# A graph network of five layers on one core: which pieces of the edge list two layers take when, and how many node steps fit beside them

## The reference, cut to what matters

```python
x = _layernorm(x + L0(x, edge_index))    # h = x + segment_sum(x[src], dst); elu(h @ W1 + b1) @ W2 + b2
x = _layernorm(x + L1(x, src, dst, ef))  # messages: mlp(x[src], x[dst], ef); segment_sum by dst; mlp
x = _layernorm(x + L2(x, edge_index))    # two SAGE layers, below
x = _layernorm(x + L3(x, W, src, dst, etypes))   # segment_sum(x[src] @ W[etype], dst), 16 types

def _sage_mean(h, src, dst, Wl, Wr, b):
    agg = segment_sum(h[src], dst)
    mean = agg / max(cnt, 1)
    return _l2norm(mean @ Wl + b + h @ Wr)
# L2: h = _sage_mean(x, first weights); batch norm over all nodes; relu;
#     out = _l2norm(_sage_mean(h, second weights) + x)
```

## Time and profile before

| | us |
|---|---|
| median of three runs | 8759.73 (8747.03 to 8762.27) |
| the profiled execution, device time | 8745.67 |
| its span | 8743.7 |
| PE busy, share of the span | 5411.1, 62% |
| POOL busy | 6302.1, 72% |
| DVE busy | 3367.5, 39% |
| ACT busy | 1499.6, 17% |
| POOL's gathers `G<-x_tab` (layer three), 1040 | 994.6 |
| POOL's gathers `G<-g_tab` (layer four), 1040 | 991.6 |

### The profile page before, as it was taken

How to read it: one execution, slowest core, us unless ns; L and a number is a source line. 1 busy time by engine, 2 the same in 40 slices (tenths; PEclk the granted TensorE clock), 3 DMA queues, 4 the chain that set the end, 5 groups by cost and what they waited for, 6 DMA issues and landing times. The chain is left out here.

```text
span 8743.7 us, 127149 instructions
## 1 busy us (share of the span) xinstructions
PE 5411.1 (62%) x29370; PEld 4179.4 (48%) x29371; DVE 3367.5 (39%) x7842; ACT 1499.6 (17%) x3432; POOL 6302.1 (72%) x6643
## 2 busy tenths in 40 slices
PE   4456766666666666667788768778877333333333
PEld 3445555555666666655555545444444222222222
DVE  3224444434444444444445434555554111111111
ACT  1111111111111111112222212233333100000000
POOL 6777777767777777767777752777766477777777
PEclk6556556557777777767878865888888555555555
DMA  3111111113333333334545424544444111111111
GB/s 79 34 34 35 35 35 34 35 37 100 97 98 97 97 98 97 99 99 110 118 111 118 113 61 128 138 145 137 140 140 117 38 30 30 30 30 30 30 30 29
DMA packets 555851, 676.47 MB, mean 77 GB/s; under 512 B 242261, under 2 KB 358003, under 8 KB 555019
## 3 DMA queue, kind: packets, MB, share of 16 engines
q0 software_dynamic: 212448, 268.01, 15.6%
q1 hardware_dynamic: 201194, 306.89, 11.8%
q10 hardware_dynamic: 141441, 93.34, 3.5%
HBM read 574.09 MB, written 93.56 MB: 76 GB/s over the span
## 5 line engine op out<-in xcount | busy, mean ns | idle before, releaser
L1919 PE MATMUL PAG<-OH,G 128*64 128x96 f32 (+1 forms) x10224 | 1573.8, 337 | 2284.0 <-DMA G<-rel_tab,IDX 984.9
L1919 PEld LDWEIGHTS PAG<-OH,G 128*64 128x64 f32 (+1 forms) x10224 | 1424.7, 204 | 2438.6 <-issue 2415.3
L1919 PE MATMUL PH<-HT 125*128 125x192 bf16 (+4 forms) x10742 | 1991.2, 314 | 303.9 <-DVE HT L1449 92.2
L832 POOL DMA_INDIRECT G<-rel_tab,IDX x1507 | 1421.8, 943 | 546.3 <-issue 459.7
L832 POOL DMA_INDIRECT G<-in_x,SRC x1525 | 1451.6, 952 | 481.9 <-issue 464.6
L832 POOL DMA_INDIRECT G<-far_tab,SRC x1527 | 1442.3, 945 | 485.0 <-issue 465.2
L1919 PEld LDWEIGHTS PH<-HT 125*128 125x128 bf16 (+4 forms) x10742 | 1275.7, 156 | 995.6 <-issue 355.2
L1411 DVE TENSOR_TENSOR AGG<-AGG,PAG 64x96 f32 (+2 forms) x852 | 211.2, 248 | 3169.0 <-PE PAG L1919 3148.1
L832 POOL DMA_INDIRECT G<-g_tab,SRC x1040 | 991.6, 953 | 582.7 <-issue 498.5
L832 POOL DMA_INDIRECT G<-x_tab,SRC x1040 | 994.6, 956 | 334.7 <-issue 315.0
L1919 PE MATMUL PAG<-OH,HT 128*128 128x96 f32 x3126 | 611.0, 376 | 524.5 <-ACT HT L1127 518.0
(11 more groups left out here) (222 smaller groups left out, 4438.9 us busy)
## 6 DMA issues: line engine op xcount, KB each, us to landing
HT<-x_parts SPq DMA_DIRECT2D x160, 468.8 KB
HT<-g_parts SPq DMA_DIRECT2D x160, 468.8 KB
GROWS<-rel_tab SPq DMA_DIRECT2D x4096, 0.2 KB
GROWS<-in_x SPq DMA_DIRECT2D x3584, 0.2 KB
HT<-src_rows SPq DMA_DIRECT2D x320, 160.0 KB
rel_tab<-STG ACTq DMA_DIRECT2D x200, 250.0 KB
GROWS<-far_tab SPq DMA_DIRECT2D x3072, 0.5 KB
GROWS<-rel_tab ACTq DMA_DIRECT2D x3072, 0.2 KB
```

Of the source, the lines that this page charges most:

```text
L832: pool.indirect_dma_start(out=G[:, h, j, 0:tabs[p].shape[1]], out_offset=None, in_=tabs[p], in_offset=bass.IndirectOffsetOnAxis(ap=numbers ...
L1919: return nc.tensor.matmul(dst, lhsT, rhs, start=start, stop=stop, skip_group_check=True)
```

## The change

Four things, all in layers three and four, and one in the preparation.

- **Order of the supers.** A new function `super_at` says which piece of the edge list a step takes: step 28 and 29 now take supers 130 and 131, and steps 130 and 131 take 28 and 29, which are "held". POOL's gathers, DVE's one-hot matrices, the window starts and SP's rows go by it. With this unit 34 has its straight edges at step 30, unit 7, which the held supers touch, has them only behind step 131, and the units below 34 and above 7 that waited for the last two supers have theirs by step 130.
- **Batches.** They are spread over 118 steps and not 126 (`supers - 14` for `supers - 6`); the last stands in step 117. The last pairs of cells are summed on PE at the start of step 118, and DVE adds the last window in step 119, behind its beats. Units that need the last window are free from step 120 and no longer only behind the last super.
- **Beat places.** Layer four has four places a step, layer three still three (`BEAT_SLOTS`). The fourth stands at the step's end, behind the second batch.
- **DVE's starts of windows** are read two at a time, every second step, in place of four every fourth.
- **Preparation.** Nine limits are checked in place of five, with nine more `link` steps, so the counts that engines wait for rise by nine.

By the new tables `rest` has 8 beats in layer three and 15 in layer four. Up to the sum of super 117 PE has in layer four 160 batches and 344 beats, where it had 150 and 326.

```diff
-ROWS_READY, COUNTED_READY, PREP_READY, TABLES_READY = 71, 85, 92, 100
+ROWS_READY, COUNTED_READY, PREP_READY, TABLES_READY = 80, 94, 101, 109
...
+HELD = 28
+HELD_UNIT = 7
...
+BEAT_SLOTS = {2: 3, 3: 4}
...
+def super_at(p, s):
+    if p not in CELL_LAYERS:
+        return s
+    early = SUPERS_OF[p] - 2
+    return {HELD: early, HELD + 1: early + 1, early: HELD, early + 1: HELD + 1}.get(s, s)
...
-        due = min(total, -(-total * (s + 1) // (supers - 6)))
+        due = min(total, -(-total * (s + 1) // (supers - 14)))
...
-            needs[u] = (min(at, supers), windows)
-            free[u] = at if at < supers else supers
+            if u < HELD_UNIT:
+                at = min(at, HELD)
+            elif u == HELD_UNIT:
+                at = supers
+            elif u == apart - 1:
+                at = HELD + 2
+            else:
+                at = min(at, supers - 2)
+            needs[u] = (at, windows)
+            free[u] = at
...
-            free[u] = step_of.get(BATCHES * windows, supers) + 1
+            free[u] = step_of.get(BATCHES * windows, LAST_BATCH_AT[p] + 2) + 1
...
-        for _ in range(3):
+        for _ in range(BEAT_SLOTS[p]):
...
# PE, cell_layer
+                    if s == LAST_BATCH_AT[p] + 1:
+                        for e in range(pairs - LAG[p], pairs):
+                            sum_cells(e)
                     beats(by_step[s][0])
...
-                for e in range(pairs - LAG[p], pairs):
-                    sum_cells(e)
+                    for now in by_step[s][3:]:
+                        beats(now)
                 beats(rest)
...
# DVE, cell_layer
+                    if s == LAST_BATCH_AT[p] + 2:
+                        add_cells(p, windows - 1, s)
+                    if s >= LAST_BATCH_AT[p] + 2:
+                        windows_before = windows
-                if windows_before:
-                    dve.wait_ge(window_added, WINDOWS_BEFORE[p] + windows_before)
+                dve.wait_ge(window_added, WINDOWS_BEFORE[p] + windows)
                 add_straight(p, supers - 1, starts[supers - 1], D)
-                add_cells(p, windows - 1, supers)
                 beats(rest)
```

More of the change, by code:

```diff
@@ L94 @@
 CELL_LAYERS = {2: (132, 35), 3: (132, 35)}
+HELD = 28
+HELD_UNIT = 7
+assert HELD % 2 == 0 and SEGMENTS[0][0] <= HELD_UNIT < SEGMENTS[0][1]
 CELL_SUPERS = SLOTS
@@ L136 @@
 BATCHES_AT = {p: batches_by_step(p) for p in CELL_LAYERS}
+LAST_BATCH_AT = {p: max(s for s, batches in enumerate(at) if batches) for p, at in BATCHES_AT.items()}
 def cell_schedule(p):
@@ L283, in gnn_kernel @@
         REGULAR_I = sb("REGULAR_I", [1, 1], I32)
-        CHECKS = sb("CHECKS", [1, 2, 5])
+        CHECKS = sb("CHECKS", [1, 2, 9])
         DST_TAB = HT[:, N - SORTED * UNITS // 2:N].bitcast(F16).rearrange("p (w u) -> p w u", u=UNITS)
@@ L711, in some_rows @@
                     if at % AT_ONCE == 0:
-                        starts[:] = row_starts(sp, row_registers, p, SP_SUPERS[p][k] // 2, e)
+                        starts[:] = row_starts(sp, row_registers, p, super_at(p, SP_SUPERS[p][k]) // 2, e)
                     row(sp, p, k % ROW_BUFS, e, starts[at % AT_ONCE])
@@ L820, in _, with gathers @@
         def _(pool):
-            def gathers(p, s, base, by_rows=()):
+            def gathers(p, s, base, by_rows=(), edges_of=None):
                 numbers = IDX3 if p == 4 else SRC
@@ L828, in gathers @@
                     pool.wait_ge(summed, base + s + 1)
-                filled = GROUP - 1 if s in by_rows else filled_chunks(s)
+                t = s if edges_of is None else edges_of(p, s)
+                filled = GROUP - 1 if s in by_rows else filled_chunks(t)
                 for j in range(filled):
-                    c = s * GROUP + j
+                    c = t * GROUP + j
                     pool.indirect_dma_start(
@@ L835, in gathers, with layers @@
                     ).then_inc(gathered[h], 16 * (GROUP - j if j == filled - 1 else 1))
-            def layers(supers, base, rows):
+            def layers(supers, base, rows, edges_of=None):
                 for p in range(LAYERS):
@@ L848, in layers @@
                     for s in range(0 if p else SHARED, supers[p]):
-                        gathers(p, s, base[p], rows[p])
+                        gathers(p, s, base[p], rows[p], edges_of)
             even, even_base = [SUPERS] * LAYERS, [SUPERS * p for p in range(LAYERS)]
@@ L860, in _ @@
             with pool.If(regular > 0):
-                layers(SUPERS_OF, BASE, by_rows)
+                layers(SUPERS_OF, BASE, by_rows, super_at)
             with pool.If(regular < 1):
@@ L1284, in _ @@
             link(nc.vector.tensor_reduce(CHECKS[:, 0, 1:2], HT[0:1, 0:SORT_SUPERS], AX.X, ALU.max))
-            limits = [COLS - 1, 0] + [UNIT * apart - 1 for _, apart in CELL_LAYERS.values()] + [P]
+            limits = [COLS - 1, 0] + [UNIT * (apart - k) - WIN for _, apart in CELL_LAYERS.values() for k in (0, 1)]
+            limits += [UNIT * (HELD_UNIT + 1) - WIN, -UNIT * HELD_UNIT, P]
             for k, (supers, _) in enumerate(CELL_LAYERS.values()):
-                link(nc.vector.tensor_reduce(CHECKS[:, 0, 2 + k:3 + k], SPANS[0:1, 0:supers], AX.X, ALU.max))
+                link(nc.vector.tensor_reduce(CHECKS[:, 0, 2 + 2 * k:3 + 2 * k], FIRST[0:1, 0:supers], AX.X, ALU.max))
+                link(nc.vector.tensor_reduce(CHECKS[:, 0, 3 + 2 * k:4 + 2 * k], FIRST[0:1, 0:supers - 2], AX.X, ALU.max))
+            held = CHECKS[:, 0, 6:8]
+            link(nc.vector.tensor_reduce(held[:, 0:1], FIRST[0:1, HELD:HELD + 2], AX.X, ALU.max))
+            link(nc.vector.tensor_reduce(held[:, 1:2], FIRST[0:1, HELD:HELD + 2], AX.X, ALU.min))
+            link(nc.vector.tensor_scalar_mul(held[:, 1:2], held[:, 1:2], -1.0))
             for k, limit in enumerate(limits):
@@ L1359, in _ @@
             dve.wait_ge(prep_products, MOST_COUNTED)
-            link(nc.vector.tensor_reduce(CHECKS[:, 0, 4:5], MOST_P, AX.X, ALU.max))
+            link(nc.vector.tensor_reduce(CHECKS[:, 0, 8:9], MOST_P, AX.X, ALU.max))
             link(nc.vector.tensor_tensor(CHECKS[:, 0, :], CHECKS[:, 1, :], CHECKS[:, 0, :], ALU.subtract))
@@ L1840, in cell_layer @@
                 for s in range(supers):
-                    if s % SLOTS == 0:
-                        for k, w0 in enumerate(starts_of(dve, registers[s // SLOTS % 2], s)):
-                            starts[s + k] = w0
+                    if s % 2 == 0:
+                        pair = registers[s // SLOTS % 2][s % SLOTS:s % SLOTS + 2]
+                        starts[s], starts[s + 1] = starts_of(dve, pair, super_at(p, s))
                     if s:
@@ L1848, in cell_layer @@
                     if s + 1 < supers:
-                        one_hot((s + 1) % 2, DREL[:, s + 1, :]).then_inc(onehot_ready, 1)
+                        one_hot((s + 1) % 2, DREL[:, super_at(p, s + 1), :]).then_inc(onehot_ready, 1)
                     beats(by_step[s][0])
```

## The result

The changed kernel takes 8790.23 us (median of 5), the kernel before 8759.73: ratio 1.0038, 95% interval 1.0026 to 1.0049, so 33 us slower by the ratio and 30.5 by the medians. 8778 was predicted, within 8720 to 8812. The profiled execution has a span of 8770.5 us, 26.8 more than before; at 8772.3 us it is the fastest of the five, 18 under their median. Where these come from is read from the first gather of each layer (timeline, POOL alone, start and length in us) and from the addition of super 117's sum.

A forecast was written before the change was run, and what follows sets the result against it. POOL was taken to set the pace in layer three, PE in layer four; +1.5 - 20 - 37.3 + 74 = +18 us gave 8764 beside the profiled 8746, 8778 beside the median, range 8720 to 8812.

The forecast's parts named there:

- What bounds layer four: Layer four: PE sets the pace, with POOL waiting 75.1 us for slots that PE has not emptied.
- the second rival: Layer four: PE has room, so the 74 us of added work are nearly free: -56, 8704 us; chance 0.05.
- The ends: Ends of layers three and four: fewer units behind the last sum and POOL's pace in layer four gain 20 and 37.3 us.
- What is paid ahead of super 117's sum: Layer four up to that sum: batches, units, waits, edge rows and stores cost 74 us, bounds 20 and 120.
- waits that the new pattern adds: Layer four: roots on ACT ahead of the next batch's copies make PE wait, net 12 us, bounds -15 and +45.
- half of 19 x 3: Layer four: PE stands about 3 us in 19 steps with no batch between, at the clock's upper level; half is 28.
- The fifth rival: Layer four: ACT's roots and stores hold up batch copies, price 115 us for 74: +59, 8819 us; chance 0.09.
- Ten batches at 4.2 us: Layer four: ten more batches on PE ahead of super 117's sum cost 42 us, 37 if none waits.
- Edge rows: Layer four: PE's waits for rows that SP fetches grow by 5 us, bounds -20 and +25.
- Windows: Layer four: most of PE's 26.1 us of waits for window additions on DVE go.
- Stores: Layer four: units following sooner make ACT wait for stores of maps, 3 us more, bounds 0 to 20.
- Prologue: Ahead of the first sum: nine more small DVE steps cost 1.5 us, between 0.5 and 2.7.

The follow-up runs named there:

- e4: The changed kernel with a root in a step's first beat place in layer four moved behind the first batch's copies on ACT: 8786.12 us, ratio 1.0038 to before.
- e6: The changed kernel with no roots or flip (beats 2 to 5) in layer four's fourth place: 8788.47 us, ratio 1.0043 to before.
- e11: The changed kernel with three beat places for four in steps 103 to 117 of layer four: 8766.54 us, ratio 1.0013 to before.
- e2: The changed kernel with three beat places a step for four in layer four, batches still over 118 steps: 8737.76 us, ratio 0.9984 to before.
- e3: The changed kernel with layer four's batches over 126 steps again and three beat places: 8751.22 us, ratio 0.9992 to before.
- e1: The changed kernel with layer four's batches over 126 steps again, four beat places kept: 8786.08 us, ratio 1.0036 to before.
- e9: As e2, but DVE reads window starts by fours where no held super is in the group: 8736.59 us, ratio 0.9981 to before.
- e10: As e2, but with four beat places in layer four from step 118 on: 8743.33 us, ratio 0.9980 to before.
- e5: The kernel before with layer three's change alone, layer four's order and end as before: 8740.90 us, ratio 0.9986 to before.

## Why the prediction came out as it did

- **What bounds layer four** held: PE sets the pace there (POOL's waits 75.1 to 174.6 us), so the second rival, free work, fell; in layer three the moved batches cost nothing. By the Trainium skill (Perfetto Trace Analysis, Identifying the Most-Contended Engine) the engine with the highest occupancy is the one to optimize first, and TensorE's headroom is judged by its weight loads, among others. This trace does not agree in layer four: POOL, busy 842 of 1272 us, waits 174.6 us for PE, whose weight loads take 578.
- **The ends** held: -22.6 for -20, and -43.2 for -37.3. Units follow at the same 18.23 us (6863.03 less 6844.80), and POOL has the pace from super 118 on.
- **What is paid ahead of super 117's sum** came out at 94.7 for 74, inside the bounds, but its parts are other ones. The term that failed is "waits that the new pattern adds ... net 12". Taking the fourth place away gives 47 us with early batches and 39 with late ones, and only 6 of its beats stand ahead of that sum (6 us by the forecast's own 7.5 a unit). The waits for copies alone grew by 56 us, on average 2.70 in the 19 steps for the 1.5 that "half of 19 x 3" took. The fifth rival named these waits and their size (3 us a step) and had a chance of 0.09; its stores did not come, for ACT waits 7.5 us for them (20.1 before), and its 115 does not follow from its own terms, since 3 us in 29 steps and 2 in 20 stores are 127 beside the 59 for batches and units.
- Its reason was half right. The roots do stand ahead of the copies, but freeing the copies gives nothing: in e4 PE waited for XS instead, and in e6 PE's waits fell to those of three places while its own work took longer at a lower clock. Nor is it shown that the chain in two steps is what costs: by the tables 29 of 41 units have beats 1 to 5 in two steps before, too, and in e6 all 43 stand as the commonest 23 of those 41 do. About half of the price lies behind the sum of super 102 (e11), where PE's stops differ by 2 us and its busy time by 19. So that the fourth place costs 39 to 47 us is shown; how much of it is the chain and how much the clock stays open. The forecast had no term for the clock.
- **Ten batches at 4.2 us** are not confirmed ahead of the sum: there the profiles have 41 us (e2 over e3) and 10 us (the changed kernel over e1), each with 11 beats beside them. Behind it they were wrong: 62 and 40 us come back, not 11.6 for batches. Net, early batches are free as far as the intervals tell. The forecast's own net for them was 42 - 11.6, some 30 us less what they do for the end; the ratios have 2 us with four places and -7 with three.
- **Edge rows** were put at +5; their waits fell by 22 us. **Windows** were to fall by most of 26; they fell by 4. Both were taken from steps whose pattern changed, and a wait is not carried from one pattern to another. **Stores** were put at +3; ACT's waits for them fell by 13.
- **Prologue**: +1.5 forecast; the profile has -2.2 to layer three, no more than two executions of the kernel before differ there (3879.1 and 3876.4).

The forecast and the result agree in sign and within 12 us, then, partly because two errors of opposite sign met: too much for batches, too little for the fourth place. The best versions measured keep the change but for that place: e2 and e9, 8738 and 8737 us, 0.9984 and 0.9981, a little faster than both kernels. e10, with the place behind the last batch alone, and e5, with layer three's change alone, are level with them.

## What to carry to other kernels

Work moved ahead of a point on a bound engine should be priced on both sides of the point in one go: what it costs ahead, and what the stretch behind it, with its clock and its tail, gives back. When stages of one unit are pressed into fewer steps, ask how much of the unit's own chain is left without other work beside it. A wait in one engine's queue that looks like the cause can move to the next link when it is taken away (e4), and a waiting engine freed of its waits can take longer for the same work at a lower clock (e6): put its busy time and its clock beside its waits. Before a difference between two profiles of a stretch is explained, see how far two executions of the same instructions lie apart there.

## What was not expected of the hardware

The granted clock of a stretch differs between executions of the same instructions: 0.83 and 0.79 over some 1070 us of layer four in e2 and e10, and 28 us with it. In the stretch behind the sum of super 117 the kernel before had 0.83 and 0.77, and e3, with four more beats there and less waiting (26 us of 155 for 30 of 130), 0.65:

```profile
6638.90:6793.70 154.80, 128.32 (x526) 72.13 (x525) 62.02 (x186) 41.29 (x109) 84.10 (x89) 0.65 0.32 90
```

What made the clock lower there stays open, as it does for the four places in the stretch behind the sum of super 102.
